# The last row of a layer in a two-layer attention kernel: denominators straight from the probabilities, and two additions moved from GpSimd to VectorE

## The chip, the cores and the metric

The kernel runs on one core of one Trainium2 chip. The time is that of one execution on the device, in microseconds (us); the lower, the better. Engines: PE is TensorE, PEld its weight loads, DVE is VectorE, ACT is ScalarE, POOL is GpSimd, SP is SyncE; ACTq and SPq are the queues from which ACT and SP issue transfers.

## The reference, cut to what matters

The input holds 128 rows of 256 tokens with 256 channels. Two layers follow each other, of the same form:

```python
x = x + attention(group_norm(x))      # layer 0
x = x + attention(group_norm(x))      # layer 1, with a mask on the keys

def attention(z):                     # each of the 128 rows by itself, 8 heads of 32 channels
    q, k, v = z @ Wq * scaling, z @ Wk, z @ Wv
    weights = softmax(q @ k.T + bias)         # 256 x 256 for each head, over the keys
    avg = weights @ v
    return (sigmoid(z @ Wg + gate_bias) * avg) @ Wo + bo
```

`group_norm` takes mean and variance of 8 channels over all rows and tokens, so layer 1 can begin only when every row of layer 0 has given its sums.

## The kernel before, in words

Everything is written by hand for each engine, with semaphores. A `Row` is a row of a layer; `slots` runs a software pipeline over them: in slot `s` the rows `s+2` down to `s-5` are each in another stage. The slots 8 to 123 are a hardware loop that is unrolled four times (`turns` is then a register); the first and the last slots are written out with plain numbers. After slot 127 no new row enters: slots 128 to 132 are the tail of a layer, in which only the last rows are finished, row 127 in slots 129 to 132.

For row `r` of the pipeline:

- PE multiplies queries and keys into `exp_bank`, two heads at a time in turn with DVE, which adds the bias (`logits`, L669) and writes `probs`. ACT takes the exponential in place (L439 in layer 1, L442 in layer 0), for four heads (one "group" `g`) and one of the two key tiles `t` at a time.
- POOL adds the two key tiles of a group: `key_sum` (L415) writes `probs_sum`. PE multiplies `probs` by the values (`average`, L770, into `av_bank`), then `probs_sum` by ones (L777, into `den_bank`), which gives the denominators. Group 0 of row `r` is done in slot `r+3`, group 1 in slot `r+4`.
- In slot `r+4` DVE forms `avg` from the gate and `av_bank` (L682), turns the denominators, inverts them and turns them back (L687, L691, L696). POOL multiplies `avg` by `recip` into `gated` (L388), and ACT rounds it to f16, `gated_hi` (L547). The instruction for `gated_hi` stands behind those of row `r-1` that store the finished row (L534) and take its squares (L539).
- In slot `r+5` POOL forms the f16 rest, `gated_lo` (L369). PE multiplies by the output weights (`output`, L797, twelve matmuls into `proj_a`), ACT adds the bias (`attn`, L508), POOL adds the residual (`y`, L382), and ACT's queue stores `y` (L534). In layer 0 ACT also takes the sum of squares of `y` (L539) with one sum for each half; the last of these releases the normalisation of layer 1.
- ACT's queue loads the residual `y` of a row (L481) in slot `r+4`, ahead of `attn` of row `r-1`. It waits there until the store of row `r-2` has landed, since `y` has two buffers.

In the tail of layer 0 SP also loads the biases of layer 1, 2 MB each (`bias_q` L299, `bias_k` L306), as soon as the last row is through with the old ones.

POOL's order in a slot is: `gated_lo` of `s-5`, `key_sum` of `s-3` group 0, the low halves of `q` and `k` of `s`, `y` of `s-5`, `gated` of `s-4`, `key_sum` of `s-3` group 1, `x_lo` of `s+1`.

Of the kernel before, what the change touches and what calls it, by code (L numbers as in the profile page):

```python
# [33 lines left out]
ROWS, TOK, CH, HEADS, HC = 128, 256, 256, 8, 32  # L34
P = 128
CT = CH // P
TT = TOK // P
# [25 lines left out]
class Row:  # L63
# [7 lines left out]

    def active(self):
        return not isinstance(self.turns, int) or 0 <= self.off < ROWS

    def index(self):

# [37 lines left out]
def build(nc, a, out):  # L114
# [11 lines left out]
    with ctx:  # L126
# [18 lines left out]
        ones = sb("ones", [P, HC], f32)  # L145
# [206 lines left out]
        @block.gpsimd  # L352
        def _(pool):
            pool.memset(ones[:, :], 1.0).then_inc(zeroed, 1)
            for m in range(2):
                pool.wait_ge(zeroed, m + 1)
                pool.memset(stack[m][MASK_ROW:P, :, :, :], 0.0).then_inc(zeroed, 1)
            pool.wait_ge(zeroed, 3)
            pool.wait_ge(const_in, 96)
            pool.tensor_scalar(half_gate_bias[:, :, :], gate_bias[:, :, :], 0.5, 1.0, ALU.mult, ALU.mult  # L360
                               ).then_inc(gate_bias_ready, 1)

            def slot(s):
                r = s.plus(-5)
                if r.active():
                    b = r.ring(2)
                    wait(pool, out_psum, r.plus(-2).count(1, 1))
                    wait(pool, gated_hi_ready, r.count(1, 1), pool_passed)
                    pool.tensor_tensor(gated_lo[:, b], gated[:, b], gated_hi[:, b], ALU.subtract  # L369
                                       ).then_inc(gated_lo_ready, 1)  # L370
                r = s.plus(-3)
                if r.active():
                    key_sum(r, 0)
                if s.active():
                    low_half(s, 0)
                    low_half(s, 1)
                r = s.plus(-5)
                if r.active():
                    i = r.ring(2)
                    wait(pool, res_in[i], r.lap(2, 16, 16))  # L380
                    wait(pool, out_left, r.count(1, 1), pool_passed)
                    pool.tensor_tensor(y[:, i], y[:, i], attn[:, i], ALU.add).then_inc(y_ready, 1)  # L382
                r = s.plus(-4)
                if r.active():
                    b = r.ring(2)
                    wait(pool, avg_ready, r.count(1, 1))
                    wait(pool, recip_ready, r.count(1, 1), pool_passed)
                    pool.tensor_tensor(gated[:, b].rearrange("p g t -> p (g t)"), avg[:, :, :].rearrange("p g t -> p (g t)"),  # L388
                                       recip[:, :], ALU.mult).then_inc(gated_ready, 1)
                r = s.plus(-3)  # L390
                if r.active():
                    key_sum(r, 1)
                r = s.plus(1)
                if r.active():
                    i = r.ring(2)
                    wait(pool, x_norm_ready, r.count(1, 1))
                    wait(pool, g_psum, r.plus(-2).count(1, 1))
                    wait(pool, v_psum, r.plus(-2).count(1, 1))
                    wait(pool, x_hi_ready, r.count(1, 1), pool_passed)
                    pool.tensor_tensor(x_lo[:, i], x_norm[:, i], x_hi[:, i], ALU.subtract).then_inc(x_lo_ready, 1)  # L400

            def low_half(r, m):
                b = r.ring(2)
                wait(pool, qk_f32_ready[m], r.count(1, 1), pool_passed)
                wait(pool, qk_hi_ready[m], r.count(1, 1), pool_passed)
                q = r.plus(-2)
                wait(pool, stack_in[q.ring(4)], stack_full(q), pool_passed)
                pool.tensor_tensor(qk_lo[m][:, b], qk_f32[m][:, b], qk_hi[m][:, b], ALU.subtract  # L408
                                   ).then_inc(qk_lo_ready[m], 1)

            def key_sum(r, g):
                wait(pool, probs_ready, r.count(4, 2 * g + 2), pool_passed)
                wait(pool, den_psum, r.plus(-1).count(2, g + 1), pool_passed)
                pr = probs[:, r.ring(2), 4 * g:4 * (g + 1)]
                pool.tensor_tensor(probs_sum[:, g], pr[:, :, 0, :], pr[:, :, 1, :], ALU.add).then_inc(sum_ready, 1)  # L415

            for l in range(2):
                slots(pool, l, slot)
# [3 lines left out]
        def _(act):  # L422
# [21 lines left out]
            def split(r, m):  # L444
                b = r.ring(2)
                ps = (pa, pb)[m]
                scale = (SCALING if m == 0 else 1.0) / W_SCALE
                act.wait_ge(qk_psum[m], r.count(1, 1))
                q = r.plus(-2)
                wait(act, stack_in[q.ring(4)], stack_full(q))  # L450
                wait(act, qk_lo_ready[m], r.plus(-2).count(1, 1))
                act.activation(qk_hi[m][:, b], ps[:, :, :], ACT.Copy, scale=scale).then_inc(qk_hi_ready[m], 1)  # L452
                act.activation(qk_f32[m][:, b], ps[:, :, :], ACT.Copy, scale=scale).then_inc(qk_f32_ready[m], 1)  # L453

            def slot(s):
                l = s.layer
# [67 lines left out]
                if r.active():  # L524
                    i = r.ring(2)
                    act.wait_ge(x_norm_ready, r.count(1, 1))
                    wait(act, g_psum, r.plus(-2).count(1, 1))
                    wait(act, v_psum, r.plus(-2).count(1, 1))
                    act.activation(x_hi[:, i], x_norm[:, i], ACT.Copy).then_inc(x_hi_ready, 1)  # L529
                r = s.plus(-5)  # L530
                if r.active():
                    i = r.ring(2)
# [2 lines left out]
                    if l == 0:  # L535
# [3 lines left out]
                            op = act.activation(attn[:, i, c], y[:, i, c], ACT.Square, bias=neg_centre[:, c:c + 1],  # L539
                                                accum_out=row_square[:, c, bass.ds(r.index(), 1)])  # L540
                        op.then_inc(stats_ready, 1)
                r = s.plus(-4)
                if r.active():
                    b = r.ring(2)
                    act.wait_ge(gated_ready, r.count(1, 1))
                    wait(act, out_psum, r.plus(-2).count(1, 1))
                    act.activation(gated_hi[:, b], gated[:, b], ACT.Copy).then_inc(gated_hi_ready, 1)  # L547
                if s.active():
                    act.wait_ge(v_psum, s.count(1, 1))
                    wait(act, av_psum, s.plus(-4).count(2, 2))  # L550
# [18 lines left out]
        def _(dve):  # L569
# [91 lines left out]
            def logits(r, h):  # L661
                if h == 0 and isinstance(r.turns, int) and r.off == 0:
                    dve.wait_ge(bias_k_in, 16 * (r.layer + 1))
                dve.wait_ge(exp_psum, r.count(8, h + 1))
                if h % 4 == 0:

                    wait(dve, av_psum, r.plus(-2).count(2, h // 4 + 1))
                    wait(dve, sum_ready, r.plus(-2).count(2, h // 4 + 1))
                dve.tensor_tensor(probs[:, r.ring(2), h], exp_bank[h % 2][:, :, :], bias_k[:, h], ALU.add  # L669
                                  ).then_inc(logits_ready, 1)  # L670

# [22 lines left out]
            def turn_reciprocal(r):  # L694
# [2 lines left out]
                              recip_part[:, :].unsqueeze(2).broadcast_to([P, HG * TOK // HC, HC])  # L697
                              ).then_inc(recip_ready, 1)

            def slot(s):  # L700
                l = s.layer
                for step in range(8):
                    if s.plus(-1).active():
                        maxima(s.plus(-1), step)
                    if step == 3 and s.plus(-4).active():
                        turn_denominator(s.plus(-4))
                    h = (step + EXP_LAG) % 8
                    r = s.plus(-3 if step < 8 - EXP_LAG else -2)
                    if r.active():
                        logits(r, h)  # L710
                    if step == 1 and s.plus(-2).active():
                        fine_shift(s.plus(-2))
                    r = s.plus(-4)
                    if r.active():
                        if step == 2:
                            gated_average(r)
                        if step == 3:
                            invert(r)
                        if step == 4:
                            turn_reciprocal(r)  # L720

            for l in range(2):
                normalisation(l)
# [4 lines left out]
        def _(pe):  # L728
# [33 lines left out]
            def average(r, g):  # L762
# [7 lines left out]
                        op = pe.matmul(av_bank[HC * j:HC * (j + 1), g, :], v_sb[:, r.ring(4), t, HC * h:HC * (h + 1)],  # L770
                                       probs[:, r.ring(2), h, t, :], start=(t == 0), stop=(t == TT - 1))
                op.then_inc(av_psum, 1)
                pe.wait_ge(sum_ready, r.count(2, g + 1))
                if g == 0:
                    wait(pe, den_left, r.plus(-1).count(1, 1))
                for j in range(4):
                    op = pe.matmul(den_bank[HC * j:HC * (j + 1), g, :], ones[:, :], probs_sum[:, g, j, :],  # L777
                                   start=True, stop=True)
                op.then_inc(den_psum, 1)

            def maxima_rows(r):
# [131 lines left out]
```

## Time and profile before

| | |
|---|---|
| runs of the kernel | 3712.91 us median of 3 (3711.34 to 3713.08) |
| profiled execution, its time | 3713.87 us |
| its span, first to last instruction | 3712.1 us |
| mean granted TensorE clock | 0.993 of 2.4 GHz |
| busy share of the span | PE 94%, DVE 93%, POOL 81%, ACT 78% |
| tail of layer 0 | about 1871 to 1921 us of the span |
| tail of layer 1 | about 3664 to 3710 us of the span |

Busy time is the time in which an engine had an instruction under way. A time in brackets behind an instruction of the timeline is how long its engine sat idle before it, and the instruction that ended that. An x count is how many instructions a line stands for; an f32 matmul counts as two.

### The profile page before, as it was taken

The numbers are of one execution on the slowest core, as the hardware profiler recorded it, in microseconds if no ns is written. First come the engines' busy times: TensorE is split into PE (matmuls) and PEld (weight loads), VectorE is DVE, ScalarE is ACT, GpSimd is POOL, SyncE is SP. The second block draws the span as 40 slices with busy tenths as digits, with TensorE's granted clock in tenths as the row PEclk, the third lists the DMA queues.
The fourth block names the chain that finished last, engine by engine and source line by source line (L and its number), as shares of the span: only waits on it lengthen the run. The fifth ranks groups of instructions, "written<-read, shape, count | busy, mean of one in ns | idle before, by whom it ended". The sixth has DMA issues, their size and how long they took to land.

```text
span 3712.1 us, 122419 instructions
## 1 busy us (share of the span) xinstructions
PE 3487.4 (94%) x36360; PEld 2625.9 (71%) x36360; DVE 3470.5 (93%) x11689; ACT 2890.9 (78%) x5393; POOL 3022.9 (81%) x2056
## 2 busy tenths in 40 slices
PE   0499999999999999999969999999999999999997
PEld 0377777777777777777747777777777777777775
DVE  6599999999999999999959999999999999999997
ACT  0388888888888888888857777778777777777785
POOL 1288888888888888888857888888888888888887
PEclk9999999999999999999989999999999999999999
DMA  8555555555555555555535556566556665566653
GB/s 319 176 117 117 116 115 117 114 119 116 116 115 116 117 117 116 115 118 114 117 112 112 118 117 118 116 121 119 117 117 119 117 121 117 117 118 117 119 119 76
DMA packets 450645, 454.09 MB, mean 122 GB/s; under 512 B 42880, under 2 KB 445440, under 8 KB 445968
## 3 DMA queue, kind: packets, MB, share of 16 engines
q1 hardware_dynamic: 241680, 251.85, 38.3%
q10 hardware_dynamic: 208896, 201.38, 19.6%
q8 instruction: 37, 0.61, 0.1%
q14 instruction: 32, 0.26, 0.0%
HBM read 182.39 MB, written 67.24 MB: 67 GB/s over the span
## 4 chain that ended last, share of the span: by engine, by line
PE 92%; DVE 3%; DMA 3%; issue 1%; POOL 1%; SPq 1%; ACT 1%; DVEq 0%; POOLq 0%; ACTq 0%
PE proj_b L743 19%; PE proj_a L743 18%; PE av_bank L770 13%; PE max_bank L754 13%; PE exp_bank L759 12%; PE proj_a L797 9%; PE den_bank L777 6%; PE proj_b L788 2%; DMA bias_k<-in_xT 1%; DVE stats L589 1%; DMA k_stack<-k_lo 1%; DVE max_bank L656 1%; DVE probs L669 0%; SPq L334 0%; POOL probs_sum L415 0%
## 5 line engine op out<-in xcount | busy, mean ns | idle before, releaser
L656 DVE CUSTOM_DVE_ANT_0 max_bank<-max_bank,bias_q 128x256 f32<-128x256 f32 x4096 | 1643.8, 443 | 156.4 <-PE max_bank L754 132.5
L415 POOL TENSOR_TENSOR probs_sum<-probs 128x1024 f32<-128x1024 f32 x512 | 1208.2, 2360 | 291.2 <-ACT probs L439 152.5
L669 DVE TENSOR_TENSOR probs<-exp_bank,bias_k 128x512 f32<-128x512 f32 x2048 | 1391.7, 680 | 7.4 <-PE exp_bank L759 7.4
L754 PE MATMUL max_bank<-k_stack,q_stack 96*128 96x256 f16 (+1 forms) x4096 | 788.0, 273 | 13.9 <-DMA k_stack<-k_lo 11.9
L759 PE MATMUL exp_bank<-q_stack,k_stack 100*128 100x256 f16 x4096 | 783.2, 272 | 9.6 <-DVE probs L669 6.3
L439 ACT ACTIVATE probs<-probs,mask_bias 128x1024 f32<-128x1024 f32 x512 | 572.8, 1148 | 61.4 <-DVE probs L669 61.2
L656 DVE DVE_READ_ACCUMULATOR2_ANT row_max<- 128x1 f32 x4096 | 573.1, 140 | 0.0
L442 ACT ACTIVATE probs<-probs 128x1024 f32<-128x1024 f32 x512 | 524.7, 1053 | 51.4 <-DVE probs L669 51.4
L770 PE MATMUL av_bank<-probs,v_sb 128*32 128x256 f32 x8192 | 549.3, 386 | 3.1 <-ACT probs L439 1.6
L754 PEld LDWEIGHTS max_bank<-k_stack,q_stack 96*128 96x128 f16 (+1 forms) x4096 | 381.2, 98 | 166.0 <-DVE row_max L656 104.3
L759 PEld LDWEIGHTS exp_bank<-q_stack,k_stack 100*128 100x128 f16 x4096 | 394.2, 97 | 72.6 <-DVE probs L669 11.5
L382 POOL TENSOR_TENSOR y<-y,attn 128x512 f32<-128x512 f32 x256 | 328.1, 1282 | 124.0 <-ACT attn L508 77.7
L400 POOL TENSOR_TENSOR x_lo<-x_norm,x_hi 128x512 f16<-128x512 f32 x256 | 299.3, 1169 | 142.2 <-ACT x_hi L529 142.2
L388 POOL TENSOR_TENSOR gated<-avg,recip 128x512 f32<-128x512 f32 x256 | 327.5, 1279 | 86.1 <-DVE recip L696 62.5
L770 PEld LDWEIGHTS av_bank<-probs,v_sb 128*32 128x32 f32 x8192 | 214.1, 109 | 199.8 <-issue 81.9
L777 PE MATMUL den_bank<-probs_sum,ones 128*32 128x256 f32 x4096 | 316.7, 381 | 5.4 <-POOL probs_sum L415 5.4
L408 POOL TENSOR_TENSOR q_lo<-q_f,q_hi 128x512 f16<-128x512 f32 x256 | 296.7, 1159 | 28.0 <-ACT q_f L453 28.0
L452 ACT ACTIVATE k_hi<-proj_b 128x512 f16<-128x512 f32 x256 | 152.9, 597 | 213.3 <-PE proj_b L743 213.3
L408 POOL TENSOR_TENSOR k_lo<-k_f,k_hi 128x512 f16<-128x512 f32 x256 | 297.2, 1161 | 12.6 <-ACT k_f L453 3.8
L369 POOL TENSOR_TENSOR gated_lo<-gated,gated_hi 128x512 f16<-128x512 f32 x256 | 298.1, 1165 | 1.8 <-ACT gated_hi L547 1.8
L494 ACT ACTIVATE x_norm<-x_in,shift_x,rstd 128x256 f32<-128x256 f32 x512 | 278.4, 598 | 7.2 <-DMA x_in<-in_xT 6.8
L551 ACT ACTIVATE v_sb<-proj_a 128x512 f32<-128x512 f32 x256 | 153.1, 598 | 163.9 <-PE proj_a L743 156.9
(132 smaller groups left out, 7049.9 us busy)
## 6 DMA issues: line engine op xcount, KB each, us to landing
q_stack<-q_hi SPq DMA_DIRECT2D x512, 128.0 KB
k_stack<-k_hi SPq DMA_DIRECT2D x512, 128.0 KB
x_in<-in_xT ACTq DMA_DIRECT2D x128, 256.0 KB, 2.7
q_stack<-q_lo SPq DMA_DIRECT2D x256, 128.0 KB
k_stack<-k_lo SPq DMA_DIRECT2D x256, 128.0 KB
y<-in_xT ACTq DMA_DIRECT2D x128, 256.0 KB, 2.9
layer_out<-y ACTq DMA_DIRECT2D x128, 256.0 KB, 2.7
x_in<-layer_out ACTq DMA_DIRECT2D x128, 256.0 KB, 2.7
```

The costliest lines, as they stand in the source:

```text
L408: pool.tensor_tensor(qk_lo[m][:, b], qk_f32[m][:, b], qk_hi[m][:, b], ALU.subtract).then_inc(qk_lo_ready[m], 1)
L415: pool.tensor_tensor(probs_sum[:, g], pr[:, :, 0, :], pr[:, :, 1, :], ALU.add).then_inc(sum_ready, 1)
L439: act.activation(pr, pr, ACT.Exp, bias=mask_bias[:, bass.ds(r.index(), 1), t]).then_inc(probs_ready, 1)
L442: act.activation(pr, pr, ACT.Exp).then_inc(probs_ready, 1)
L656: op = dve.tensor_tensor_reduce(out=max_bank[h % 2][:, t, :], in0=max_bank[h % 2][:, t, :], in1=bias_q[:, h, t, :], scale=1.0 / FINE, scal ...
L669: dve.tensor_tensor(probs[:, r.ring(2), h], exp_bank[h % 2][:, :, :], bias_k[:, h], ALU.add).then_inc(logits_ready, 1)
L743: op = pe.matmul(ps[:, tile, :], lhs, rhs, start=(n == 0), stop=(n == len(terms) - 1))
L754: op = pe.matmul(bank_[:, t, :], q[0:n, t * P:(t + 1) * P], k[0:n, :], start=True, stop=True)
L759: op = pe.matmul(bank_[:, t, :], k[0:n, t * P:(t + 1) * P], q[0:n, :], start=True, stop=True)
L770: op = pe.matmul(av_bank[HC * j:HC * (j + 1), g, :], v_sb[:, r.ring(4), t, HC * h:HC * (h + 1)], probs[:, r.ring(2), h, t, :], start=(t == ...
L777: op = pe.matmul(den_bank[HC * j:HC * (j + 1), g, :], ones[:, :], probs_sum[:, g, j, :], start=True, stop=True)
L797: op = pe.matmul(pa[:, o, :], w[l][:, e, o * P:(o + 1) * P], g[:, b, e, :], start=(n == 0), stop=(n == len(terms) - 1))
```

## The change

For the last row of each layer alone (`r.last()`, off 127):

- `key_sum` falls away on POOL. PE multiplies both key tiles of `probs` by ones and lets PSUM add them: eight f32 matmuls for a group in place of four. PE no longer waits for `sum_ready`; POOL raises that semaphore by two at the place of the second sum, so that the counts stay right.
- `gated` and `gated_lo` (`last_gated`) and the residual sum `y` (`last_residual`) are done by DVE, not by POOL, in DVE's slots 131 and 132 at step 4.

In every tail slot (128 to 131) of both layers ACT's `gated_hi` of row `s-4` stands ahead of the store and the squares of row `s-5`, not behind them. For every row, in the loop too, DVE's logits wait for `den_psum` of row `r-2` in place of both `av_psum` and `sum_ready` of that row: one wait less, twice in a row.

```diff
@@ pool slot
-                if r.active():
+                if r.active() and not r.last():
...
-                if r.active():
+                if r.last():
+                    pool.sem_inc(sum_ready, 2)
+                elif r.active():
                     key_sum(r, 1)
@@ scalar slot
+            def high_gated(r):
+                if r.active():
+                    b = r.ring(2)
+                    act.wait_ge(gated_ready, r.count(1, 1))
+                    wait(act, out_psum, r.plus(-2).count(1, 1))
+                    act.activation(gated_hi[:, b], gated[:, b], ACT.Copy).then_inc(gated_hi_ready, 1)
...
+                if not s.active():
+                    high_gated(s.plus(-4))
                 r = s.plus(-5)
                 if r.active():
                     i = r.ring(2)
                     wait(act, y_ready, r.count(1, 1), act_passed)
                     act.dma_start(channel_major(dst[l], r.index() * TOK, TOK), y[:, i]).then_inc(y_out[i], 16)
...
+                if s.active():
+                    high_gated(s.plus(-4))
@@ vector logits
-                    wait(dve, av_psum, r.plus(-2).count(2, h // 4 + 1))
-                    wait(dve, sum_ready, r.plus(-2).count(2, h // 4 + 1))
+                    wait(dve, den_psum, r.plus(-2).count(2, h // 4 + 1))
@@ vector
+            def last_gated(r):
+                b = r.ring(2)
+                dve.wait_ge(avg_ready, r.count(1, 1))
+                dve.wait_ge(recip_ready, r.count(1, 1))
+                dve.tensor_tensor(gated[:, b].rearrange("p g t -> p (g t)"), avg[:, :, :].rearrange("p g t -> p (g t)"),
+                                  recip[:, :], ALU.mult).then_inc(gated_ready, 1)
+                dve.wait_ge(out_psum, r.plus(-2).count(1, 1))
+                dve.wait_ge(gated_lo_ready, r.plus(-1).count(1, 1))
+                dve.wait_ge(gated_hi_ready, r.count(1, 1))
+                dve.tensor_tensor(gated_lo[:, b], gated[:, b], gated_hi[:, b], ALU.subtract).then_inc(gated_lo_ready, 1)
+
+            def last_residual(r):
+                i = r.ring(2)
+                dve.wait_ge(res_in[i], r.lap(2, 16, 16))
+                dve.wait_ge(y_ready, r.plus(-1).count(1, 1))
+                dve.wait_ge(out_left, r.count(1, 1))
+                dve.tensor_tensor(y[:, i], y[:, i], attn[:, i], ALU.add).then_inc(y_ready, 1)
@@ tensor average
-                pe.wait_ge(sum_ready, r.count(2, g + 1))
+                if not r.last():
+                    pe.wait_ge(sum_ready, r.count(2, g + 1))
...
-                for j in range(4):
-                    op = pe.matmul(den_bank[HC * j:HC * (j + 1), g, :], ones[:, :], probs_sum[:, g, j, :],
-                                   start=True, stop=True)
+                parts = [probs[:, r.ring(2), 4 * g:4 * (g + 1), t, :] for t in range(TT)] if r.last() else [probs_sum[:, g]]
+                for t, part in enumerate(parts):
+                    for j in range(4):
+                        op = pe.matmul(den_bank[HC * j:HC * (j + 1), g, :], ones[:, :], part[:, j, :],
+                                       start=(t == 0), stop=(t == len(parts) - 1))
```

## Rows read from the trace of the kernel before

**Rows 1.** Page, first part: busy time, share, instructions of each engine.
```profile
PE 3487.4 (94%) x36360; PEld 2625.9 (71%) x36360; DVE 3470.5 (93%) x11689; ACT 2890.9 (78%) x5393; POOL 3022.9 (81%) x2056
```

**Rows 2.** Windows: stretch, length, busy PE PEld DVE ACT POOL, PEclk, DMA, GB/s.
```profile
2800.00:3650.00 850.00, 844.64 (x8880) 639.20 (x8881) 823.81 (x2814) 674.05 (x1124) 733.86 (x500) 1.00 0.60 118
...
3690.00:3696.00 6.00, 2.62 (x40) 0.78 (x32) 1.48 (x3) 2.87 (x4) 5.69 (x4) 0.92 0.28 90
3696.00:3698.00 2.00, 1.88 (x12) 1.20 (x9) 1.60 (x3) 0.00 (x0) 0.24 (x1) 0.50 0.01 4
```

**Rows 3.** Timeline of the loop, VectorE: start, length, engine, line, op.
```profile
1008.00 0.14 DVE L656 DVE_READ_ACCUMULATOR2_ANT row_max<- 128x1 f32 x1
1008.00 0.69 DVE L669 TENSOR_TENSOR probs<-exp_bank,bias_k 128x512 f32<-128x512 f32 x1
```

**Rows 4.** Groups by form: out<-in, shapes, count | busy, mean ns | idle.
```profile
L669 DVE TENSOR_TENSOR probs<-exp_bank,bias_k 128x512 f32<-128x512 f32 x2048 | 1391.7, 680 | 7.4 <-PE exp_bank L759 7.4
...
L382 POOL TENSOR_TENSOR y<-y,attn 128x512 f32<-128x512 f32 x256 | 328.1, 1282 | 124.0 <-ACT attn L508 77.7 <-issue 46.3
...
L589 DVE BATCH_NORM_STATS2 stats<-probs 128x512 f32 x64 | 38.7, 678 | 15.2 <-DMA probs<-in_xT 15.2
```

**Rows 5.** Chain that ended last, end of layer 0: start, length, what.
```profile
1905.40 2.73 PE proj_a L797 x12
...
1908.16 1.03 ACT attn L508 x4
...
1914.10 2.73 PE proj_a L797 x12
```

**Rows 6.** Timeline, end of layer 0.
```profile
1893.09 2.01 ACT L442 ACTIVATE probs<-probs 128x1024 f32<-128x1024 f32 x2
...
1898.07 1.07 PE L770 MATMUL av_bank<-probs,v_sb 128*32 128x256 f32 x16
...
1898.80 0.33 SPq L306 DMA_DIRECT2D bias_k<-in_bias_k  x1
...
1900.57 1.28 POOL L388 TENSOR_TENSOR gated<-avg,recip 128x512 f32<-128x512 f32 x1
1900.64 0.39 ACTq L534 DMA_DIRECT2D layer_out<-y  x1
1901.08 0.51 ACT L539 ACTIVATE attn<-y,neg_centre 128x256 f32<-128x256 f32 x1
...
1907.40 0.38 ACTq L481 DMA_DIRECT2D y<-in_xT  x1
...
1912.80 1.15 POOL L369 TENSOR_TENSOR gated_lo<-gated,gated_hi 128x512 f16<-128x512 f32 x1 [1.00 <-ACT gated_hi L547]
```

**Rows 7.** DMA issues with us to landing; landing of the 1900.64 store.
```profile
bias_k<-in_bias_k SPq DMA_DIRECT2D x1, 2048.0 KB, 8.1
...
DMA to landing us min/median/max: 6.7/6.7/6.7
```

**Rows 8.** Timeline, end of layer 1; last row of it from the chain.
```profile
3691.53 1.28 POOL L388 TENSOR_TENSOR gated<-avg,recip 128x512 f32<-128x512 f32 x1
3691.61 0.39 ACTq L534 DMA_DIRECT2D out<-y  x1
...
3692.29 1.07 PE L770 MATMUL av_bank<-probs,v_sb 128*32 128x256 f32 x16 [1.57 <-ACT probs L439]
...
3692.85 0.63 ACT L547 ACTIVATE gated_hi<-gated 128x512 f16<-128x512 f32 x1 [0.61 <-POOL gated L388]
...
3693.78 0.37 ACTq L481 DMA_DIRECT2D y<-layer_out  x1
...
3695.18 1.08 PE L777 MATMUL den_bank<-probs_sum,ones 128*32 128x256 f32 x8 [1.81 <-POOL probs_sum L415]
...
3698.86 0.84 ACT L508 ACTIVATE attn<-proj_a,out_bias 128x256 f32<-128x256 f32 x2 [5.38 <-PE proj_a L797]
...
3704.43 2.73 PE proj_a L797 x12
```

More of the change, by code:

```diff
@@ L73, in active, with last @@
         return not isinstance(self.turns, int) or 0 <= self.off < ROWS
+    def last(self):
+        return isinstance(self.turns, int) and self.off == ROWS - 1
     def index(self):
@@ L371, in slot @@
                 r = s.plus(-3)
-                if r.active():
+                if r.active() and not r.last():
                     key_sum(r, 0)
@@ L377, in slot @@
                 r = s.plus(-5)
-                if r.active():
+                if r.active() and not r.last():
                     i = r.ring(2)
@@ L383, in slot @@
                 r = s.plus(-4)
-                if r.active():
+                if r.active() and not r.last():
                     b = r.ring(2)
@@ L390, in slot @@
                 r = s.plus(-3)
-                if r.active():
+                if r.last():
+                    pool.sem_inc(sum_ready, 2)
+                elif r.active():
                     key_sum(r, 1)
@@ L541, in slot @@
                         op.then_inc(stats_ready, 1)
[L542 to L547, printed above, removed]
+                if s.active():
+                    high_gated(s.plus(-4))
                 if s.active():
@@ L720, in slot @@
                             turn_reciprocal(r)
+                        if step == 4 and r.last():
+                            last_gated(r)
+                    r = s.plus(-5)
+                    if step == 4 and r.last():
+                        last_residual(r)
             for l in range(2):
```

## The prediction

> **What bounds the kernel now.** I read the page's busy shares first, then windows, then the chain that ended last and the timeline at the two layer ends, then the DMA issues. By the page PE and DVE are both above 90% busy [rows 1]; which of them sets the time is to be read stage by stage. In a long stretch of the loop PE is busy 844.64 of 850 us, DVE 823.81 [rows 2]: PE is the bound there, and DVE, POOL and ACT have slack. In the tails that is over. From 3690 to 3696 PE works 2.62 of 6 us while POOL works 5.69 [rows 2], and the chain runs from engine to engine. Its links in layer 0: the output matmuls of row 126 (1905.40, 2.73 long), their `attn` (1908.16, 1.03), and the output matmuls of row 127 at 1914.10 [rows 5]. In layer 1 the same: PE waited 1.81 us for `probs_sum` before the last denominators at 3695.18, `attn` of row 126 came at 3698.86, and row 127's output started at 3704.43 [rows 8]. PE is at its lower clock there (PEclk 0.50 from 3696 to 3698 [rows 2], 1.2 GHz), so twelve output matmuls take 2.73 us; at the upper level half of that, 1.37. So what the change can be worth lies in two stretches of some 10 us, and each microsecond taken off the chain in one counts once, since layer 1 cannot begin before layer 0's last squares.
>
> **The loop.** The change takes one wait of DVE away, twice in a row of the loop. I cost it at nothing, for two reasons: PE is the bound, and DVE does not feel its waits: the logits with three waits (L669 at 1008.00) start with no gap behind the instruction before [rows 3], and all 2048 of L669 together had 7.4 us of idle time before them, all of it for PE [rows 4]. If that cover were gone, those 7.4 us are the most that could come back. The new condition, `den_psum` of row r-2, is not late either: by the order of `slots` those matmuls were issued seven steps before group 0's logits and eight before group 1's, nearly a whole slot.
>
> **What happens before slot 131.** `gated_hi` now goes ahead of the store and the squares. The store of row 125 left at 1900.64; now ACT's queue stands at the wait for `gated` of row 126, which POOL ends at 1900.57 + 1.28 = 1901.85 [rows 6]: 1.25 us later in layer 0, in layer 1 from 3691.61 to 3692.85 alike [rows 8]. Queued behind it are the squares of the row before, the exponentials of the next slot, the load of the next `y`, and `attn`. In layer 0's slot 129 the squares of row 124 (two halves of 0.51 and their sums) are pushed behind `gated_hi`, and the exponentials of row 127, group 0 (1893.09, 2.01 [rows 6]) slip by about 1.0, to 1896.1. PE takes them at 1898.07 [rows 6]: hidden, by 2 us.
>
> **Layer 1, step by step** [rows 8, 6, 5]. Hand-overs: 0.04 us to ACT (1.28 behind 3691.53 is 3692.81, ACT starts at 3692.85) and 0.15 to PE (1912.80 + 1.15 is 1913.95, PE at 1914.10); I use 0.04 for DVE and 0.15 for POOL too.
> - POOL no longer has the second sum in its way, so `gated_lo` of row 126 follows `gated_hi` (3692.85 + 0.63 = 3693.48): 3693.63 to 3694.78.
> - PE: `average` of row 127 at 3692.29, 16 passes in 1.07. The denominators follow at once, again 16 passes, so 1.07: done by 3694.4. The sum on POOL (2.3 long) is gone, the four extra matmuls cost 0.5 and lie in what was waiting. Output of row 126 starts at 3694.93 and not at 3696.4. PE is then idle for only 0.5 us before it, where it was idle for 1.8, so I take the upper clock: 1.37, end 3696.3 (at the lower clock 3697.7: my upper bound).
> - ACT: the load of `y` of row 127 waits for the store of row 125, which took 2.17 (3691.61 to 3693.78): 3692.87 + 2.17 = 3695.04, no obstacle. `attn` 3696.4, 0.84 long: 3697.25. `gated_hi` of row 127, 0.63: 3697.9. DVE has `gated` ready by then: 3694.4, three instructions of at most 0.7 each for the inverse, and 0.7 for the product: 3697.2 at the latest.
> - DVE subtracts: no instruction of DVE with these operands is in the trace. Floor: L669, 128x512 f32 with two inputs, 680 ns; ceiling: POOL's own y add, 1282 ns [rows 4]. I take 0.68, since DVE's length follows the elements (L589, one input from SBUF, 678). `gated_lo` ends at 3698.6, PE starts at 3698.8 and not at 3704.43: **5.65 us**.
> - `y` on DVE: 1.28 becomes 0.68: **0.6 us**. Layer 1 gives 6.25.
>
> **Layer 0, step by step** [rows 5, 6, 7]. The output of row 126 would start at about 1903.95 (1901.85, 0.04, 0.63, 0.15, 1.15, 0.15) and end by 1906.7 even at the lower clock. But what is late next is not PE: the load of `y` of row 127 sits in ACT's queue ahead of `attn` of row 126, and went only at 1907.40. It waits for the store of row 125, which took 6.7 us, for the 2 MB of `bias_k` were under way from 1898.80 to 1898.80 + 8.1 = 1906.9. The store lands 0.4 us behind them. I take it that its own later issue does not move that (floor), and 1.25 more as the ceiling. So `attn` goes at 1907.40 + 0.44 (as 1901.08 stands to 1900.64) = 1907.84 and not at 1908.16: 0.3 of the 1.5 that PE offers. Then `attn` 1.03, `gated_hi` 0.63, DVE 0.04 + 0.68, PE 0.15: output of row 127 at 1910.35 and not at 1914.10, **3.75 us**; POOL's y add of row 126, POOL's product and the squares of row 126 are no longer between. `y` gives **0.6**. Layer 0: 4.35.
>
> The Trainium skill, DMA: Bandwidth & Descriptors, § Queues, rings and completion order, says that a DMA's semaphore increment lands only after every earlier write of the same engine, whatever queue it came from. The trace agrees: 6.7 us, ending with `bias_k`. By it the store's landing stays at 1907.4; without it, and with 2.17 us as in layer 1, `attn` could go at 1906.7 and the sum would be 1.1 us more.
>
> **Sum.** 4.35 + 6.25 = 10.6 us. Against the profiled execution: span 3712.1 to 3701.5, its time 3713.87 to 3703.3. The median, 3712.91, lies 1.0 below that execution: **3702.3**.
>
> **The rivals.**
> - *The two engines get in each other's way.* DVE's `gated_lo` of row 127 falls in POOL's y add of row 126, which starts 0.15 behind `attn`: in layer 1 3697.4 to 3698.7, DVE wants to start at 3697.95. If the second waits for the first, PE starts 0.75 later, in layer 0 likewise: 1.5 us, 3703.8. For it: both read f32 from SBUF, and DVE reads two such inputs, which no DVE row of the tail or loop does. Against it: L669 with one such input takes 680 ns beside a busy POOL, L589 678 at the start. The Trainium skill, SBUF — State Buffer, § SBUF: two separate sides, gives it as a rule: a DVE instruction with two SBUF inputs and a GpSimd instruction that reads SBUF exclude each other. No row here has that pair, so I can't say that the trace agrees.
> - *The late store and the low clock.* The store of row 125 in layer 0 carries its delay on (1.25), and layer 1's output of row 126 stays at the lower clock (1.35): 2.6 less, 3704.9; with the rival above 3706.4.
> - *It does not do what it says.* The holding back of the store and the load takes the place of the sum in both layers: `attn` of row 126 would come no sooner than before, and only what lies between it and the last output is won less a second wait: some 3 us per layer, 3707. The 1907.40 row speaks for it in layer 0; in layer 1 the 2.17 us of the store speak against it.
> - *Faster still.* The loop's lighter waits give back part of the 7.4 us, or the store lands early: 2 to 4 us more, 3699.
> - *Slower.* The new wait holds DVE in the loop. It would need the denominators of row r-2 to be seven steps late; DVE's slack there is 26 of 850 us, so beyond 0.035 us of added wait for each of the 512 waits with PE made to follow, 18 us in all, the time ends 0.2% above: 3720.3. The 7.4 us and the gapless row 1008.00 speak against it.
>
> **Chances.** What this measurement can tell from no change is about 0.2%, 7.4 us; so faster means below 3705.5. Forecast 0.4; engines in each other's way 0.27; late store or low clock, alone or with it, 0.14 (a third of it above 3705.5); does not do what it says 0.07; faster still 0.09; slower 0.03. Faster: 0.4 + 0.27 + 0.09 + 0.09 = 0.85; within 0.2%: 0.12; slower 0.03. Range: from 3699.5 (a part of the faster case) to 3706.5 (the rivals' sum), which leaves out 0.2 at most.
>
> **What would show it.** In the profile after: no L415 for row 127; the last denominators right behind the last `av_bank` matmuls; output of row 126 in layer 1 in about 1.4 us; in layer 0 the load of `y` still at about 1907.4 with `attn` 0.44 behind; from the start of `attn` of row 126 to that of row 127's output 2.5 us in each layer, not 5.9 and 5.6; the DVE subtraction 0.68 long and starting within 0.1 of the end of `gated_hi`, or, if the first rival holds, with the end of POOL's add; loop windows unchanged in PE's share. The forecast is wrong if the loop's period moves, or if a store's landing decides in layer 1 too.

## The result and the profile after

Over 12 runs each, the changed kernel takes 3704.90 us (3700.89 to 3706.89), the kernel before 3713.41 us (3711.34 to 3716.08): 8.5 us less, ratio 0.9976, 95% interval 0.9967 to 0.9985. Forecast were 3702.3 us and 10.6 us of gain, with a range of 3699.5 to 3706.5. The profiled execution took 3704.79 us with a span of 3703.0, where the one before had 3712.1: 9.1 less. The lines of the functions have moved; the helper for the high half is L465 now, DVE's product, remainder and residual are L713, L718 and L725.

Busy shares on the page as in [rows 1], then windows at the same places as [rows 2]:

```profile
PE 3485.5 (94%) x36392; PEld 2625.8 (71%) x36392; DVE 3477.0 (94%) x11695; ACT 2893.6 (78%) x5393; POOL 3005.7 (81%) x2046
```

```profile
2800.00:3650.00 850.00, 845.22 (x8877) 640.46 (x8875) 824.66 (x2816) 675.36 (x1124) 733.93 (x500) 1.00 0.59 118
3690.00:3696.00 6.00, 3.40 (x44) 2.04 (x44) 3.34 (x6) 2.01 (x5) 2.56 (x3) 1.00 0.27 89
3696.00:3698.00 2.00, 0.83 (x8) 0.78 (x9) 1.02 (x1) 0.00 (x0) 0.47 (x1) 1.00 0.28 98
```

The loop is as it was: PE 845.22 of 850 us. In layer 1's tail the stretch from 3690 has PE busy for 3.40 us, not 2.62, and POOL for 2.56, not 5.69; and from 3696 to 3698 the granted clock is 1.00 (2.4 GHz) where it was 0.50. The places are the same but not the work in them: this tail starts 2.2 us earlier, so the last window had the output of row 126 before and has the first matmuls of the output of row 127 now.

The timeline at the end of layer 0, to be laid beside [rows 5, 6]:

```profile
1901.18 0.63 ACT L465 ACTIVATE gated_hi<-gated 128x512 f16<-128x512 f32 x1 [0.80 <-POOL gated L391]
1901.19 0.39 ACTq L548 DMA_DIRECT2D layer_out<-y  x1
...
1904.29 0.69 DVE L713 TENSOR_TENSOR gated<-avg,recip 128x512 f32<-128x512 f32 x1
...
1907.31 0.38 ACTq L493 DMA_DIRECT2D y<-in_xT  x1
1907.80 0.47 ACT L520 ACTIVATE attn<-proj_a,out_bias 128x256 f32<-128x256 f32 x1 [5.01 <-DMA layer_out<-y]
...
1908.72 0.62 ACT L465 ACTIVATE gated_hi<-gated 128x512 f16<-128x512 f32 x1
1908.96 1.26 POOL L385 TENSOR_TENSOR y<-y,attn 128x512 f32<-128x512 f32 x1 [5.86 <-ACT attn L520]
1909.47 1.30 DVE L718 TENSOR_TENSOR gated_lo<-gated,gated_hi 128x512 f16<-128x512 f32 x1 [4.49 <-ACT gated_hi L465]
...
1910.92 0.58 PE L832 MATMUL proj_a<-gated_hi,w_out_hi 128*128 128x256 f16 x2 [6.20 <-DVE gated_lo L718]
...
1914.83 0.69 DVE L725 TENSOR_TENSOR y<-y,attn 128x512 f32<-128x512 f32 x1 [4.05 <-ACT attn L520]
```

The store of row 125 (1901.19) leaves right behind POOL's product of row 126, and no longer behind POOL's y add of row 125. DVE's product is done at 1904.98. The load of `y` of row 127 still goes only at 1907.31, `attn` of row 126 stands 0.49 behind it, the high half behind `attn`. Then DVE's remainder: 1.30 long, where DVE's product and residual of the same size take 0.69. It begins at 1909.47, inside POOL's y add (1908.96 to 1910.22), and ends 0.55 behind it.

The DMA issue of `bias_k` with its us to landing, and the landing of the 1901.19 store, as in [rows 7]:

```profile
bias_k<-in_bias_k SPq DMA_DIRECT2D x1, 2048.0 KB, 8.6
```

```profile
DMA to landing us min/median/max: 6.1/6.1/6.1
```

The load was issued at 1898.10, so it landed at 1906.7, the store at 1907.3.

The timeline at the end of layer 1, beside [rows 8], and two pieces of its chain:

```profile
3690.07 1.07 PE L802 MATMUL av_bank<-probs,v_sb 128*32 128x256 f32 x16 [1.14 <-ACT probs L444]
...
3690.96 1.05 PE L812 MATMUL den_bank<-probs,ones 128*32 128x256 f32 x16
...
3691.42 1.16 POOL L372 TENSOR_TENSOR gated_lo<-gated,gated_hi 128x512 f16<-128x512 f32 x1 [0.81 <-ACT gated_hi L465]
...
3692.82 0.38 ACTq L493 DMA_DIRECT2D y<-layer_out  x1
...
3694.23 0.84 ACT L520 ACTIVATE attn<-proj_a,out_bias 128x256 f32<-128x256 f32 x2 [2.96 <-PE proj_a L832]
...
3695.21 1.26 POOL L385 TENSOR_TENSOR y<-y,attn 128x512 f32<-128x512 f32 x1 [2.63 <-ACT attn L520]
3695.72 1.30 DVE L718 TENSOR_TENSOR gated_lo<-gated,gated_hi 128x512 f16<-128x512 f32 x1 [1.09 <-ACT gated_hi L465]
...
3699.64 0.69 DVE L725 TENSOR_TENSOR y<-y,attn 128x512 f32<-128x512 f32 x1 [2.62 <-ACT attn L520]
3700.37 0.39 ACTq L548 DMA_DIRECT2D out<-y  x1
```

```profile
3692.72 1.48 PE proj_a L832 x12
...
3697.17 1.49 PE proj_a L832 x12
```

The denominators of row 127 follow `average` at once (3690.96, 16 passes in 1.05); the output of row 126 takes 1.48 us in place of 2.46. DVE's remainder is 1.30 here too, beside POOL's add from 3695.21 to 3696.47. The output of row 127 takes 1.49, not 2.73.

To compare tails of different runs I measure from the start of `attn` of row 125 to the first statistics instruction of layer 1 (layer 0's tail) or to the last store's issue (layer 1's). Before: 1898.17 to 1920.87, 22.70, and 3689.33 to 3709.45, 20.12. After: 1897.47 to 1917.12, 19.65, and 3687.11 to 3700.37, 13.26. So the tails gave 3.05 and 6.86 us, 9.91 together. The 0.8 us that the span does not show were lost elsewhere. ACT writes a tile `coarse` once for each row, which makes a good marker. The slot from that of row 126 to that of row 127, ahead of the part that was changed, took 14.24 us in layer 1, not 12.92, and 13.65 in layer 0, not 14.18. Over the kernels below this slot lies between 12.84 and 14.24, with the same work in it: 12.84 and 12.93 where the granted clock was 1.00 throughout, anything from 12.92 to 14.24 where it fell for a part (0.87 to 0.92 on average). So a difference of a microsecond between two spans says nothing. The tail lengths are the better measure, though not exact either: two profiles of the changed kernel differ by 0.39 and 0.71 us in them (below).

### The profile page after: what moved, and what is told of

Its sections match the earlier page's. It is cut to its first block, busy times and chain, and to the rows that moved or that the text cites. A ratio compares the mean times of both kernels' runs of the same rounds, so it can differ in the third digit from the quotient of the medians.

```text
span 3703.0 us, 122184 instructions
## 1 busy us (share of the span) xinstructions
PE 3485.5 (94%) x36392; PEld 2625.8 (71%) x36392; DVE 3477.0 (94%) x11695; ACT 2893.6 (78%) x5393; POOL 3005.7 (81%) x2046
## 4 chain that ended last, share of the span: by engine, by line
PE 91%; DMA 3%; DVE 3%; issue 1%; POOL 1%; ACT 1%; SPq 0%; DVEq 0%; ACTq 0%; POOLq 0%
PE proj_b L775 19%; PE proj_a L775 18%; PE av_bank L802 13%; PE max_bank L786 13%; PE exp_bank L791 12%; PE proj_a L832 9%; PE den_bank L812 6%; PE proj_b L823 2%; DVE stats L599 1%; DMA bias_k<-in_xT 1%; DMA k_stack<-k_lo 1%; DMA probs<-in_xT 1%; DVE max_bank L666 1%; DVE probs L678 0%; SPq L337 0%
```

## Experiments

Each kernel ran beside the kernel before on the same chip. Medians are in us, "tails" are the two lengths above, layer 0 and layer 1 (before 22.70 and 20.12, changed 19.65 and 13.26). The edits are shown against the kernel before in the first four and against the changed kernel behind them; `...` marks what is left out, and the comments in them are mine.

| kernel | this | before beside it | ratio, 95% interval | tails |
|---|---|---|---|---|
| wait alone | 3713.78 | 3714.85 | 0.9996 (0.9987 to 1.0005) | 22.51, 20.41 |
| denominators alone | 3711.78 | 3714.85 | 0.9992 (0.9983 to 1.0001) | 22.49, 17.71 |
| high half alone | 3714.59 | 3714.85 | 1.0002 (0.9993 to 1.0011) | 22.51, 20.23 |
| DVE alone | 3712.05 | 3714.85 | 0.9994 (0.9985 to 1.0003) | 21.66, 18.21 |
| residual 126 held | 3704.61 | 3715.87 | 0.9972 (0.9960 to 0.9983) | 18.71, 12.98 |
| load behind | 3700.97 | 3715.87 | 0.9961 (0.9947 to 0.9974) | 16.60, 13.25 |
| bias load held | 3704.52 | 3715.87 | 0.9970 (0.9959 to 0.9981) | 15.35, 13.26 |
| high half first | 3702.54 | 3715.87 | 0.9966 (0.9952 to 0.9979) | 17.08, 13.72 |
| changed, again | 3704.48 | 3715.34 | 0.9972 (0.9962 to 0.9982) | 19.26, 13.97 |
| load behind and held | 3700.43 | 3715.34 | 0.9959 (0.9945 to 0.9972) | 15.96, 12.97 |
| high half first, load behind | 3700.32 | 3715.34 | 0.9961 (0.9947 to 0.9975) | 15.92, 12.55 |

**The loop's wait alone.** The kernel before with only this edit:

```diff
-                    wait(dve, av_psum, r.plus(-2).count(2, h // 4 + 1))
-                    wait(dve, sum_ready, r.plus(-2).count(2, h // 4 + 1))
+                    wait(dve, den_psum, r.plus(-2).count(2, h // 4 + 1))
```

> The kernel before with one edit: DVE's logits wait for den_psum of row r-2 and not for av_psum and sum_ready. My theory: PE is the bound in the loop and DVE never feels these waits, so the time is that of before within 1 us. Rival: the loop carries part of the gain of the whole change (8.5 us); then this kernel is 2 to 7 us faster and its row period in the loop (13.5 us) is shorter. Second rival: the new wait holds DVE; then it is slower.

No measurable change. The mean row of the loop (from one `coarse` to another, 106 rows on in layer 0 and 98 in layer 1) is 13.609 and 13.608 us before, 13.606 and 13.607 here: some 0.5 us in all 256 rows. Both rivals fall.

**The denominators alone.**

```diff
+                if r.last():
+                    pool.sem_inc(sum_ready, 2)        # no key_sum for row 127
...
+                parts = [probs[:, r.ring(2), 4 * g:4 * (g + 1), t, :] for t in range(TT)] if r.last() else [probs_sum[:, g]]
```

> The kernel before with the denominators of row 127 from both key tiles (and the den_psum wait that this needs), nothing else. By the chain: in layer 1 GpSimd's remainder of row 126 starts 1.45 us earlier and all behind it with it, 1.5 to 2.8 us (the larger if PE is at its upper clock for the output of row 126); in layer 0 the load of y, which waits for the landing of a store behind bias_k, lets through 0.3. Together 1.8 to 3 us faster. Rival: there is no such hold in layer 0, then 3 to 5 us faster.

This kernel has the loop's edit too, since its denominators need that wait. The tails are 0.21 and 2.41 shorter, 2.6 together, within what was expected. Layer 0 gives nearly nothing (the wait alone has 0.19 there) although the same POOL sum is gone from both: there the load of `y` holds `attn`.

**The high half alone.**

```diff
+                if not s.active():
+                    high_gated(s.plus(-4))            # ahead of store and squares
```

> The kernel before with the high half ahead of store and squares in the tail slots, nothing else. In layer 0 the high half of row 127 no longer stands behind the squares of row 126, which cost it 0.25 us; in layer 1 there are no squares. Expected: 0.2 us faster, so no measurable change. Rival: the store held back by 1.25 us in every tail slot costs something on its own; then 1 to 3 us slower.

0.19 shorter in layer 0, as expected, and 0.11 longer in layer 1: nothing that a time could show. The later store costs nothing by itself.

**The three DVE instructions alone.**

```diff
+                        if step == 4 and r.last():
+                            last_gated(r)
...
+                    if step == 4 and r.last():
+                        last_residual(r)
```

> The kernel before with product, remainder and residual of row 127 on DVE, nothing else. Layer 0: the high half still stands behind the squares of row 126, so only the shorter remainder (0.5) and y (0.6) count; layer 1: the product no longer stands behind GpSimd's y of row 126, 1.25, and 0.5 and 0.6: together 3.4 us faster. GpSimd is idle beside DVE's remainder here, so it should take 0.69 us if it was the neighbour that stretched it to 1.30 in the changed kernel, and 1.30 if that is its own length for these operands (then 2.3 us faster).

1.04 and 1.91 shorter, 2.95 together; DVE's remainder, from the timeline at the end of layer 0:

```profile
1910.74 0.69 DVE L714 TENSOR_TENSOR gated_lo<-gated,gated_hi 128x512 f16<-128x512 f32 x1 [4.90 <-ACT gated_hi L463]
```

POOL's y add of row 126 had ended at 1908.53. The length is 0.69, so 1.30 is not the instruction's own. The expectation was 0.45 too high, in layer 1: the high half waited there for the store's issue behind POOL's add. The three parts alone sum to 5.7 us of tail (2.62, 0.08, 2.95), the whole has 9.9. Most of the rest is the way from `attn` of row 126 to the high half of row 127. It takes 3.89 us in layer 0 and 3.50 in layer 1 before, 3.68 and 3.50 with the high half moved, 3.89 and 2.77 with DVE's product, and 0.92 and 0.73 with both. With the high half moved it still waits for POOL's product, which stands behind POOL's y add of row 126; with DVE's product it still stands behind the store and the squares, which wait for the same add. Only the two together get past it.

**The residual sum of row 126 held.**

```diff
                     wait(pool, out_left, r.count(1, 1), pool_passed)
+                    if r.plus(1).last():
+                        pool.wait_ge(gated_lo_ready, r.plus(1).count(1, 1))
```

> The changed kernel with one wait more: GpSimd begins the residual sum of row 126 only when DVE's remainder of row 127 is done. If the two shut each other out of SBUF, DVE's remainder takes 0.69 us and not 1.30, and the kernel is 1.2 us faster than the changed one (0.6 in each layer). If 1.30 is the instruction's own length, it stays at 1.30 and the time is unchanged.

Timeline at the end of layer 1:

```profile
3693.41 0.69 DVE L720 TENSOR_TENSOR gated_lo<-gated,gated_hi 128x512 f16<-128x512 f32 x1 [1.09 <-ACT gated_hi L467]
...
3694.24 0.38 PE L834 MATMUL proj_a<-gated_hi,w_out_hi 128*128 128x256 f16 x2 [2.36 <-DVE gated_lo L720]
3694.27 1.27 POOL L387 TENSOR_TENSOR y<-y,attn 128x512 f32<-128x512 f32 x1 [4.00 <-DVE gated_lo L720]
```

With POOL's add behind it, the same DVE instruction takes 0.69: it is POOL's add that made it long. From `attn` of row 126 to the output of row 127 now pass 2.50 and 2.32 us, not 3.12 and 2.94, so 0.62 is won there in each layer. In layer 0 the tail is 0.94 shorter than the changed kernel's in its first profile and 0.55 than in its second; what goes beyond or stays below 0.62 is where `attn` of row 126 came, 10.02 us behind that of row 125 against 10.33 and 9.95. In layer 1 it is only 0.28 shorter than in the first, with the upper clock in both: the store of row 126 waits for the add that was held (its issue is at 3695.57) and stands ahead of `attn` of row 127, which starts at 3696.08 and so gives 0.3 back. Expected were 1.2 us of time. By medians, each against the kernel before on its chip, there are 0.4 us: too little to be told in time, plain in the trace.

**The load of `y` behind.**

```diff
-                r = s.plus(-4)
-                if r.active():
...
-                    act.dma_start(y[:, i], channel_major(src[l], r.index() * TOK, TOK)).then_inc(res_in[i], 16)
+                if not s.plus(-4).last():
+                    load_residual(s.plus(-4))         # the lines taken out, as a function
...
                 if not s.active():
                     high_gated(s.plus(-4))
+                if s.plus(-4).last():
+                    load_residual(s.plus(-4))         # behind attn and the high half
```

> The changed kernel with the load of y for row 127 moved behind attn and the high half in slot 131, so that attn of row 126 does not stand behind the wait for the store's landing. If that landing is what holds layer 0 (the load at 1907.3, PE done at 1904.7), the kernel is 3.0 us faster than the changed one, all in layer 0. If something else holds attn there, no change.

ScalarE and its queue at the end of layer 0:

```profile
1902.91 0.47 ACT L524 ACTIVATE attn<-proj_a,out_bias 128x256 f32<-128x256 f32 x1 [1.97 <-PE proj_a L838]
...
1904.87 0.37 ACTq L474 DMA_DIRECT2D y<-in_xT  x1
```

Layer 0's tail is 3.05 shorter than the changed kernel's, layer 1's unchanged (13.25). `attn` goes as soon as PE is done, the load still waits for the landing, and nobody waits for the load. By medians 4.0 us faster than the changed kernel, each against its own kernel before (14.9 and 10.9); the 1 us beyond the tail is in no tail, and I have no cause for it.

**The bias load held.**

```diff
                     sp.wait_ge(logits_ready, 8 * ROWS)
+                    for i in range(2):
+                        sp.wait_ge(y_out[i], 16 * (ROWS // 2))
```

> The changed kernel with the 2 MB load of the key bias of layer 1 issued only when all stores of layer 0 have landed. If the store of row 125 lands late because of that load (6.1 us), it lands after about 2.2 us now, attn of row 126 goes at about 1904.8, and the kernel is 3.0 us faster than the changed one. If the store is late for another reason, its landing and the time stay. The load still lands before layer 1 needs it, so it should cost nothing.

Store of row 125, load of `y` and `attn`, end of layer 0; then a piece of the chain at the start of layer 1:

```profile
1902.16 0.39 ACTq L550 DMA_DIRECT2D layer_out<-y  x1
...
1904.33 0.37 ACTq L495 DMA_DIRECT2D y<-in_xT  x1
1905.74 0.47 ACT L522 ACTIVATE attn<-proj_a,out_bias 128x256 f32<-128x256 f32 x1 [1.97 <-PE proj_a L834]
```

```profile
1917.72 5.26 DMA x_in<-layer_out
```

The store lands in 2.1 us without `bias_k`, not 6.1: the cause is shown. Layer 0's tail is 15.35, even 4.3 shorter: 3.0 by `attn`, as with the load behind, and 1.25 because the output of row 127 had the upper clock. That second part is luck: PE was idle for 3.16 us before it in both kernels, and had the lower clock in the other (windows with the output of row 127 in layer 0, load behind first):

```profile
1906.00:1909.00 3.00, 2.72 (x12) 1.65 (x12) 0.00 (x0) 1.12 (x5) 0.00 (x0) 0.50 0.54 172
```

```profile
1908.80:1910.40 1.60, 1.47 (x12) 1.10 (x12) 0.00 (x0) 0.96 (x5) 0.00 (x0) 1.00 0.52 174
```

But "it should cost nothing" was wrong: the first load of layer 1's input took 5.26 us beside `bias_k` where it took 2.82, on the chain. From the first statistics to `coarse` of row 126 in layer 1 passed 1747.4 us, where the changed kernel has 1743.4 and the eleven others 1742.4 to 1745.8, so a part of these 4 us is drift. By medians 0.5 us were left of the gain.

**The high half of row 127 first.**

```diff
                 r = s.plus(-4)
+                if r.last():
+                    high_gated(r)                     # ahead of the load of y and of attn of row 126
...
-                if not s.active():
+                if not s.active() and not s.plus(-4).last():
                     high_gated(s.plus(-4))
```

> The changed kernel with the high half of row 127 ahead of the load of y and of attn of row 126 in slot 131. Layer 0: high half and DVE's remainder are done while ACT waits for the landing, so the output of row 127 starts right behind attn of row 126: 2.0 us earlier. Layer 1: attn of row 126 starts 1.0 later, but the output of row 127 follows it at once: 1.0 earlier. DVE's remainder lies beside no GpSimd work and takes 0.69. Together 3.0 us faster than the changed kernel. If the order on ACT is not on the chain, no change.

Layer 0: 2.57 shorter. The 2.0 expected are there (from `attn` of row 126 to the output of row 127 1.12 us, not 3.12); the other 0.56 is an earlier landing of the store. That this output ran partly at the upper clock (2.09 us) gave nothing, since `attn` of row 127 now stood behind the squares of row 126. DVE's remainder, beside no work of POOL, took 0.69 in both layers. Layer 1: 0.46 longer, not 1.0 shorter. `attn` of row 126 came 1.2 later, the output of row 127 came 0.8 earlier than in the changed kernel and ran in this window:

```profile
3694.60:3697.60 3.00, 2.72 (x12) 1.61 (x12) 0.00 (x0) 0.14 (x2) 1.26 (x1) 0.50 0.37 125
```

Its clock is 0.50, and the low level took back more than the order gained. PE's idle time does not explain it: it was 2.20 us before this output, and 2.98 in the changed kernel, which had the upper clock. By medians the gain over the changed kernel is 2.5 us, with 3.0 expected.

**The changed kernel again, and the two combinations.** Their edits are those above, together.

> The changed kernel itself, as the measure for the two beside it: 8 to 11 us faster than the kernel before on this chip.

> The changed kernel with both edits that helped alone: the load of y for row 127 behind attn and the high half, and GpSimd's residual sum of row 126 held until DVE's remainder of row 127 is done. If the two gains (3.05 in layer 0; 0.9 and 0.3 in the two layers) are of different places they add up: 4.2 us faster than the changed kernel. If the squares of row 126, now later, come in the way of attn of row 127 in layer 0, 0.5 to 1 less.

> The changed kernel with the high half of row 127 ahead of attn of row 126, and the load of y for row 127 behind it. Layer 0: attn of row 126 about 0.9 later than with the load behind alone, but the output of row 127 right at its end: 15.5 us from attn of row 125 to the last statistics, where the changed kernel has 19.65. Layer 1: 13.7 as with the high half first alone, where the low clock came back, or 12.3 at the upper clock. Together 3.7 to 5 us faster than the changed kernel.

The changed kernel repeats at 3704.48. Both combinations are 4.1 us below it on the same chip, with hardly overlapping runs (3697.83 to 3700.87 and 3696.08 to 3701.62 against 3701.38 to 3708.28). The load behind carries nearly all: alone it was 14.9 us below its kernel before, the combinations 14.9 and 15.0. What the other edits add shows in the tails (0.9 and 1.4 us less than with the load behind alone), not in the medians. In layer 0 both had the upper clock for the output of row 127 and won nothing by it: `attn` of row 127 stood behind the squares of row 126, as one of the expectations feared, 2.75 and 3.31 us after that output began. Either beats both kernels of this case, by 0.4% against the kernel before.

## Why the prediction was right, point by point

- **The loop costs and gives nothing.** Right: the wait alone changes neither the time nor the row period.
- **Layer 1, up to `attn` of row 126.** Predicted: by ending POOL's sum and by the upper clock for the output of row 126, `attn` from 3698.86 to 3696.4, 2.45 us [rows 8]. Measured against `attn` of row 125: 9.53 before, 7.12 after, 2.41. The denominators alone give the same 7.12, so this term is theirs. The upper clock that I took for this output was no luck: it takes 1.46 to 1.48 us in all 18 tails with the denominators edit, and 2.30 to 2.73 in the eight without.
- **Layer 1, from there to the store.** Predicted 3.2 for what lay between `attn` and the output of row 127 and 0.6 for `y`. Measured 2.63 (5.57 becomes 3697.17 less 3694.23, 2.94) and 0.6 (1.26 becomes 0.69). The missing 0.6 is DVE's remainder, 1.30 and not 0.68. On the other side 1.24 us came that I had not counted: the output of row 127 at the upper clock, 1.49 for 2.73. Layer 1: 6.25 forecast, 6.86 in this profile, 6.15 in the second.
- **Layer 0, the load that holds `attn`.** The place was right and so was the landing at about 1907.4 by the issue's own 0.49; load behind and bias load held show it. The 0.3 us gained there did not come. The distance of `attn` of row 126 from that of row 125 was 9.99 before, 10.33 and 9.95 in the two profiles after: `bias_k` took 8.6 us and not 8.1, and the store landed 0.6 behind it.
- **Layer 0, from `attn` to the output of row 127.** Predicted 2.5; measured 1910.92 less 1907.80, 3.12. Again the 0.62 of DVE's remainder.
- **The term that was mis-sized** is thus "I take 0.68, since DVE's length follows the elements": it measured 1.30 in both layers, above my ceiling of 1.28, and cost 1.2 us. With it the sum is 9.4, and 8.5 was measured. The rival of the engines that get in each other's way, to which I gave 0.27, is what happened: 3703.8 by it, 3704.9 measured. I had priced it from a start 0.75 later; the rows show an instruction that starts at once and is held until POOL's is over.
- **How much of it was luck.** The 10.6 less 1.2 for the remainder and 0.6 for layer 0's `attn` (0.3 gained forecast, 0.34 lost measured), plus the 1.24 that I had not counted, is 10.0; the tails gave 9.9. So the upper clock happened to pay for the remainder; without it this execution, 3704.79, would have taken some 3706.0, close to the upper end of the range. The 9.9 became 9.1 by the two slots above, and 8.5 by medians. The forecast also started from a median of three runs, 3712.91; the twelve give 3713.41.
- **A sum that does not hold.** In the rival "slower" the price has no base: 26 us of slack over the some 126 waits of that stretch is 0.2 us for each, not 0.035, and 18 us of added wait do not lead to 3720.3. Nothing hangs on it, since the row period did not move.

The Trainium skill, SBUF — State Buffer, § SBUF: two separate sides, says that a DVE instruction with two SBUF inputs and a GpSimd instruction that reads SBUF exclude each other, and that whichever starts first keeps the ports. The rows agree: POOL's add, first, keeps its 1.26; DVE's ends 0.55 behind it, and takes 0.69 when alone. Had DVE worked at half its pace beside POOL for those 0.75 us, it would have ended 0.3 behind (my estimate from these rows), so standing still fits better than sharing. Every overlap of this pair in these traces has DVE start 0.51 behind POOL; another offset, or DVE first, was not tried. The Trainium skill, DMA: Bandwidth & Descriptors, § Queues, rings and completion order, says that a semaphore increment lands only after the same engine's earlier writes of other queues. The 6.1 us beside `bias_k` and 2.1 without agree with it, and so does the 5.26 us load, which landed 0.7 behind the held `bias_k` (issued at 1914.47, 7.8 to landing); they would also agree with mere sharing of the engines, and no run here tells the two apart.

What stays open: why the output of row 127 in layer 1 got the upper clock in some profiles (1.49 here) and only for a part in others (in the second profile of the changed kernel the tail was 0.71 longer by it). In the 26 tails of these traces PE stood idle for 4.4 us or more before that output in thirteen, and the output took 2.71 to 2.73 in each. In the other thirteen it was idle for 1.9 to 3.6 us, and eight took 1.46 to 1.49, three 1.64 to 2.19, two 2.72, in no order of the idle time. So the change, which cut the idle time in layer 1 from 5.6 to 3.0 us, made the upper clock possible but not certain. I did not vary the idle time by itself.

## What to carry to other kernels

When a wait is taken out of a tail, lay the next in-order queue beside it: here `attn` stood behind a DMA issue that waited for a landing, and moving that issue behind the work gave layer 0 its share. A `tensor_tensor` with two SBUF inputs that is moved from GpSimd to VectorE gets the shorter time only if GpSimd is not adding from SBUF at that moment. Two waits for the same instruction on two paths must both go: DVE's product and the moved high half gave at most 0.7 us a layer alone and 2.8 to 3.0 together. Measure tails from a marker inside them; spans drift by more than such edits give.

## What the runs showed of the hardware

- A DVE `tensor_tensor` with both inputs in SBUF (128x512) takes 0.69 us alone and 1.30 when it starts 0.5 us into a GpSimd `tensor_tensor` of 1.26, which itself is not lengthened; DVE's logits, with one input in PSUM, keep 0.68 in a loop where GpSimd is busy 734 of 850 us.
- A 256 KB store that lands in 2.1 us took 6.1 while 2 MB were being loaded by another queue; a 256 KB load took 5.26 in the same company, 2.82 without.
- The granted clock decides about 1.2 us for twelve output matmuls (1.49 against 2.73). Idle time alone does not tell which level comes: behind the same 3.16 us two kernels had 1.00 and 0.50, and behind 2.20 us one had 0.50 where another had 1.00 behind 2.98.
